# Splitting half of the embedding product of two row tiles into three fp32r products, with GpSimd making the parts

## The reference, cut to what matters

```
x = layer_norm(patches, g1, b1)          # 448 x 1024
x = x @ W + b                            # W: 1024 x 512, all float32
h = layer_norm(x, g2, b2)                # 448 x 512
h = h + attention(normalise(h))          # 16 heads of 128, causal, 7 keys each
h = h + ffn(quantise(normalise(h)))      # fp8 quantised rows, 512 x 512
```

## Time and profile before

| | |
|---|---|
| time, three runs | 265.09 us median, 264.95 to 265.5 |
| the profiled execution | 264.66 us, span 262.9 us |
| TensorE matmul (PE) | 256.3 us busy, 97% |
| TensorE weight load (PEld) | 220.1 us, 84% |
| VectorE (DVE) | 157.6 us, 60% |
| ScalarE (ACT) | 125.0 us, 48% |
| GpSimd (POOL) | 0.2 us, 0% |
| granted TensorE clock | 0.99 |
| chain of work that ended last | PE 91%, DVE 4% |
| embedding products (L353) in that chain | 10% |

### The profile page before, as it was taken

How to read it: one execution, slowest core, us unless ns; L and a number is a source line. 1 busy time by engine, 2 the same in 40 slices (tenths; PEclk the granted TensorE clock), 3 DMA queues, 4 the chain that set the end, 5 groups by cost and what they waited for, 6 DMA issues and landing times.

```text
span 262.9 us, 3852 instructions
## 1 busy us (share of the span) xinstructions
PE 256.3 (97%) x1428; PEld 220.1 (84%) x1428; DVE 157.6 (60%) x321; ACT 125.0 (48%) x216; POOL 0.2 (0%) x4
## 2 busy tenths in 40 slices
PE   8999999999899999999999999999999999999994
PEld 6444548989799999999999999999999999998772
DVE  6367887627828623942591288139623958934884
ACT  2677853635535343624363345435333642537680
POOL 0000000000000000000000000000000000000000
PEclk9999999999999999999999999999999999999898
DMA  5999120340270233052205300530320020000004
GB/s 161 358 302 372 30 91 0 99 143 0 51 271 0 89 113 120 1 168 59 92 0 199 120 0 16 184 120 0 111 89 0 2 80 0 2 0 0 0 4 140
DMA packets 7585, 23.57 MB, mean 90 GB/s; under 512 B 1251, under 2 KB 1715, under 8 KB 7446
## 3 DMA queue, kind: packets, MB, share of 16 engines
q1 hardware_dynamic: 7574, 23.42, 26.6%
HBM read 22.50 MB, written 0.92 MB: 89 GB/s over the span
## 4 chain that ended last, share of the span: by engine, by line
PE 91%; DVE 4%; DMA 1%; issue 1%; ACT 1%; SPq 0%; DVEq 0%; ACTq 0%
PE bank L312 14%; PE bank L313 14%; PE bank L314 14%; PE acc L353 10%; PE acc L454 9%; PE bank L429 5%; PE bank L438 5%; PE acc L458 4%; PE acc L648 3%; PE bank L444 3%; PE bank L421 2%; PE bank L518 2%; PE bank L336 1%; DMA x_in<-patches 1%; PE bank L634 1%; DVE stats L949 1%
## 5 line engine op out<-in xcount | busy, mean ns | idle before, releaser
L312 PE MATMUL bank<-ht_hi,qkvw_hi 128*128 128x448 f32 (+1 forms) x192 | 69.4, 362 | 0.9 <-issue 0.9
L313 PE MATMUL bank<-ht_lo,qkvw_hi 128*128 128x448 f32 (+1 forms) x192 | 69.0, 360 | 0.0
L314 PE MATMUL bank<-ht_hi,qkvw_lo 128*128 128x448 f32 (+1 forms) x192 | 69.0, 360 | 0.0
L942 DVE TENSOR_TENSOR qkvw_lo<-raw_qkv,qkvw_hi 128x1536 fp32r<-128x1536 f32 x16 | 28.1, 1754 | 35.4 <-ACT qkvw_hi L680 35.4
L312 PEld LDWEIGHTS bank<-ht_hi,qkvw_hi 128*128 128x128 f32 x192 | 36.1, 188 | 3.9 <-issue 1.2
L314 PEld LDWEIGHTS bank<-ht_hi,qkvw_lo 128*128 128x128 f32 x192 | 36.1, 188 | 2.7
L313 PEld LDWEIGHTS bank<-ht_lo,qkvw_hi 128*128 128x128 f32 x192 | 36.1, 188 | 2.6
L353 PE MATMUL acc<-tokw_raw,xt 128*112 128x512 f32 x64 | 28.6, 592 | 0.0
L680 ACT CAST qkvw_hi<-raw_qkv 128x1536 fp32r<-128x1536 f32 x16 | 23.5, 1470 | 0.0
L1112 DVE COPY prob_t<-bank 112x448 f32<-112x448 f32 x8 | 5.0, 624 | 29.0 <-PE bank L421 29.0
L353 PEld LDWEIGHTS acc<-tokw_raw,xt 128*112 128x112 f32 x64 | 10.9, 177 | 13.7 <-issue 10.6
(11 more groups left out here) (145 smaller groups left out, 395.3 us busy)
## 6 DMA issues: line engine op xcount, KB each, us to landing
raw_qkv<-heads_w SPq DMA_DIRECT2D x16, 768.0 KB, 4.3
raw_out<-heads_w SPq DMA_DIRECT2D x16, 256.0 KB, 4.5
tokw_raw<-tok_w SPq DMA_DIRECT2D x4, 512.0 KB, 6.7
x_in<-patches SPq DMA_DIRECT2D x3, 448.0 KB, 9.3
ffnw_raw<-ffn_w SPq DMA_DIRECT2D x1, 1024.0 KB, 15.3
out<-h_sb SPq DMA_DIRECT2D x3, 224.0 KB, 2.6
x_in<-patches SPq DMA_DIRECT2D x2, 224.0 KB, 2.9
g_row<-tok_g SPq DMA_DIRECT2D x1, 224.0 KB, 10.4
```

The source lines that it names most:

```text
L312: nc.tensor.matmul(ps, hi, whi, start=first, stop=False, skip_group_check=True)
L313: nc.tensor.matmul(ps, hi, wlo, start=False, stop=False, skip_group_check=True)
L314: return nc.tensor.matmul(ps, lo, whi, start=False, stop=last, skip_group_check=True)
L942: return nc.vector.tensor_tensor(dst, src, hi.bitcast(F32), ALU.subtract)
```

## The change

GpSimd gets a stream. First it makes, for chunks 4 to 7 of the embedding weights, the high part (`tensor_copy` from float32 to fp32r) and the low part (`tensor_tensor` subtract), in two steps of two chunks (1024 elements in each of 128 partitions), each step after its quarter of the weights has landed. Then, for tile 2 and tile 3, once all eight chunks of `xt` of the tile are there, it makes the high and the low part of chunks 4 to 7 of `xt` (448 elements in each of 128 partitions). Each subtraction waits for the copy before it. The parts are put into the buffers of the feed-forward's weights and activations, which are not in use before the end.

TensorE does chunks 0 to 3 of every tile, and all of tiles 0 and 1, as before. For tiles 2 and 3, from chunk 4 on, `embed_split` takes the place of the four float32 products: eight fp32r products of the high part of `xt` with the high and low parts of the weights, then four of the low part of `xt` with the high part of the weights. It waits for the high part of the patches, for each pair of weight chunks, and before the last four for the low part of the patches.

```diff
+FIRST_SPLIT, FIRST_SPLIT_TILE = 4, 2
...
+        tokw_hi, tokw_lo = ffnw_hi, ffnw_lo
+        xt_hi, xt_lo = xq_t[:, 0:2, :], xq_t[:, 2:4, :]
...
+        @block.gpsimd
+        def _(pool):
+            def split_weights(i):
+                a, b = 2 * i, 2 * i + 2
+                pool.wait_ge(tokw_landed[(FIRST_SPLIT + a) // 2], 16)
+                raw = tokw_raw[:, FIRST_SPLIT + a:FIRST_SPLIT + b, :]
+                nc.gpsimd.tensor_copy(tokw_hi[:, a:b, :], raw).then_inc(tokw_hi_ok, 1)
+                pool.wait_ge(tokw_hi_ok, i + 1)
+                nc.gpsimd.tensor_tensor(tokw_lo[:, a:b, :], raw, tokw_hi[:, a:b, :].bitcast(F32),
+                                        ALU.subtract).then_inc(tokw_lo_ok, 1)
+
+            def split_patches(t):
+                i = t - FIRST_SPLIT_TILE
+                pool.wait_ge(xt_ok, KIN * (t + 1))
+                raw = xt[:, t % 2, FIRST_SPLIT * TR:KIN * TR]
+                nc.gpsimd.tensor_copy(xt_hi[:, t % 2, :], raw).then_inc(xt_hi_ok, 1)
+                pool.wait_ge(xt_hi_ok, i + 1)
+                nc.gpsimd.tensor_tensor(xt_lo[:, t % 2, :], raw, xt_hi[:, t % 2, :].bitcast(F32),
+                                        ALU.subtract).then_inc(xt_lo_ok, 1)
+
+            for i in range((KIN - FIRST_SPLIT) // 2):
+                split_weights(i)
+            for t in range(FIRST_SPLIT_TILE, TILES):
+                split_patches(t)
...
+            def embed_split(t):
+                pe.wait_ge(xt_hi_ok, t - FIRST_SPLIT_TILE + 1)
+                for i in range(KIN - FIRST_SPLIT):
+                    if i % 2 == 0:
+                        pe.wait_ge(tokw_hi_ok, i // 2 + 1)
+                        pe.wait_ge(tokw_lo_ok, i // 2 + 1)
+                    for w in (tokw_hi, tokw_lo):
+                        nc.tensor.matmul(acc[t][0:TR, :], xt_hi[:, t % 2, i * TR:(i + 1) * TR], w[:, i, :],
+                                         start=False, stop=False, skip_group_check=True)
+                pe.wait_ge(xt_lo_ok, t - FIRST_SPLIT_TILE + 1)
+                for i in range(KIN - FIRST_SPLIT):
+                    last = nc.tensor.matmul(acc[t][0:TR, :], xt_lo[:, t % 2, i * TR:(i + 1) * TR], tokw_hi[:, i, :],
+                                            start=False, stop=(i == KIN - FIRST_SPLIT - 1), skip_group_check=True)
+                return last
+
             def embed(t, ahead_of):
                 for k in range(KIN):
...
                     pe.wait_ge(xt_ok, KIN * t + k + 1)
+                    if t >= FIRST_SPLIT_TILE and k >= FIRST_SPLIT:
+                        last = embed_split(t)
+                        break
                     last = nc.tensor.matmul(acc[t][0:TR, :], xt[:, t % 2, k * TR:(k + 1) * TR], tokw_raw[:, k, :],
                                             start=False, stop=(k == KIN - 1), skip_group_check=True)
                 last.then_inc(tok_ps, 1)
```

More of the change, by code:

```diff
@@ L144, in audio_tower @@
         tok_b_landed = sem("tok_b_landed")
+        tokw_hi_ok = sem("tokw_hi_ok")
+        tokw_lo_ok = sem("tokw_lo_ok")
+        xt_hi_ok = sem("xt_hi_ok")
+        xt_lo_ok = sem("xt_lo_ok")
         bias_cleared = sem("bias_cleared")
```

## The result

| | before | changed |
|---|---|---|
| median of 18 runs each | 265.00 us | 264.44 us |
| lowest to highest | 264.59 to 266.08 | 263.77 to 265.42 |
| ratio, with 95% interval | | 0.9971 (0.9962 to 0.998) |
| profiled execution, span | 264.66 us, 262.9 us | 264.58 us, 262.8 us |

The changed kernel is faster, by 0.8 us by the ratio (0.5 to 1.0 us by its interval). I had forecast 264.5 us and a gain of 0.6 us.

The account below looks back on a forecast made before the run. TensorE, busy 97% of the span and 91% of the chain, was taken as the bound. A gain of 1.0 us less 0.4 us for the hold on VectorE gave -0.6 us, 264.5 us against the median, range 263.9 to 265.5 us.

Parts of the forecast that it names:

- TensorE's part: Tiles 2 and 3: twelve fp32r products replace four float32 ones, saving 0.63 us a tile, 1.26 us in all.
- Rival D: On TensorE: fp32r products go at 0.29 us each, no gain, 265.2 us with a small hold; chance 0.06.
- What is late next: At tile 3's `hn_sb` transposes: only 1.0 us of 1.26 us comes through, bounds 0.6 and 1.3 us.
- the wait between the two halves: At tile 3's `hn_sb` transposes: the second pair no longer waits for the second half of `hn_sb`, estimated 0.1 us.
- its two chains: Meeting at tile 3's `hn_sb` transposes: VectorE's for tile 3, 1.26 us earlier, and TensorE's own work, 0.63 us earlier.
- GpSimd ready in time: Parts for tiles 2 and 3 are ready before TensorE wants them, with 3 to 4 us of cover; costs nothing.
- Rival C: TensorE waits at tile 2's high part because GpSimd is too slow: +2.5 us, 267.6 us; chance 0.07.
- The hold on VectorE: GpSimd delays VectorE's small operations on tile 2's patches (17.38 to 17.99 us): 0.4 us lost, bounds 0 and 1.7.
- rival A: The hold on VectorE at tile 2's patches costs nothing: -1.0 us, 264.1 us; chance 0.31.
- B: Full hold on VectorE; TensorE stops about 1.0 us at tile 2's patch transposes: 0.0, about 265.1 us; chance 0.20.
- The sum: Whole kernel: -1.0 us for TensorE's saving and +0.4 us for the hold give -0.6 us.

Follow-up runs that it names:

- x1: Changed kernel with only tile 2 split into fp32r products, tile 3 as before: 264.76 us, 0.9983 of the kernel before.
- x2: Changed kernel with only tile 3 split into fp32r products, tile 2 as before: 264.98 us, 0.999 of the kernel before.
- x7: Changed kernel with the nine residual transposes moved ahead of tile 2's `hn_sb` transposes: 263.87 us, 0.9961 of the kernel before.
- x9: Changed kernel with GpSimd's weight steps gated, residual transposes first, and tile 3's root ahead of ScalarE's copy for tile 2: 263.56 us, 0.9958 of before.
- x4: Changed kernel with GpSimd's weight steps waiting so that none runs while VectorE makes a patch `nmr`: 264.28 us, 0.9961 of the kernel before.
- x5: The changed kernel run once more, unedited: 264.28 us, 0.9979 of the kernel before.
- x11: Kernel before, no GpSimd work, with residual transposes first, root first and tile 2's patches loaded earlier: 265.35 us, 1.001 of the kernel before.
- x3: Changed kernel where GpSimd does all its splitting but TensorE keeps the float32 products: 265.22 us, 1.0006 of the kernel before.
- x10: Changed kernel plus tile 1 split, gated weight steps, residual transposes and root first, tile 2's patches before the last weights: 263.51 us, 0.994 of before.
- x6: Changed kernel with one more GpSimd copy (616 elements) between the two weight steps: 264.59 us, 0.9988 of the kernel before.

## Why the prediction was right, point by point

**TensorE's part.** Forecast 0.61 to 0.67 us for each tile, by 0.231 us a product; 0.67 us read at tile 2, products at 0.23 us. Right. Rival D is out.

**What is late next.** The stop ahead of tile 2's `hn_sb` transposes was forecast at 0.7 us and is 0.65 us; x1 and x2 show that the two tiles are worth 0.68 and 0.32 us, where the forecast had 0.63 us and the rest of 1.0. Tile 3's transposes were forecast 0.9 us earlier and are 0.97 and 0.98 us earlier, counted from P1. The last products of the first head (47.13 us before, 46.51 us in the changed kernel) were forecast 1.0 us earlier and are: 32.51 us behind P1 before, 31.51 us now. The 0.1 us for the wait between the two halves was not there (the row of the four transposes went from 0.64 to 0.61 us). But one of its two chains was wrong: I had VectorE's for tile 3 1.26 us earlier. It starts 1.3 us earlier, counted from P1, and ends 1.0 us earlier, as it waits for a root on ScalarE that stands behind a copy, and the copy waits for the transposes of tile 2 that stand behind the very stop I had predicted. I had followed what TensorE's stop does to TensorE's own work and not to the queue of the engine that it feeds. That the number came out all the same is luck: TensorE's own work, the chain I had right, was as late. x7 is where the error showed, and x9, which moves the root, is its proof.

**GpSimd ready in time.** Forecast 1.0 to 2.0 us for the copy, 1.2 to 2.3 us for the subtraction, weights done between 16.3 and 20.6 us: 1.04 and 2.39 us, done at 18.9 us. The subtraction lies just above my upper end. No product waited. Rival C is out.

**The hold on VectorE.** Forecast 0.4 us between 0 and 1.7. That it exists is shown by seven profiled executions with it and by x4, where it is gone. The Trainium skill (SBUF — State Buffer, "Who interferes with whom") says that the second of the two "fully blocks" until the first is done, and the traces agree: the held operation ended 0.01 to 0.02 us behind GpSimd's in all seven. The slack that covers it was forecast at 1.3 us and is 4.59 - 3.37 = 1.22 us. Its price is 0 in the two profiles of the changed kernel (rival A); over the six profiles with the weight steps as in the change it is 0, 0, 0, 0.21, 0.40 and 0.43 us, 0.2 us in the mean, half of the forecast. The times would allow the 0.4 us of the forecast and cannot show it: by the medians x5 is 0.3 us worse than x4, but the intervals overlap, and x7, which has the hold, has x4's ratio. B, a stop of 1.0 us, appeared in none. What I had not seen is what sets the price: where GpSimd's last weight step ends against P1, which depends on when the third quarter of the weights lands (the first copy started between 11.65 and 12.76 us) and on how early TensorE is. The prediction's reckoning with a subtraction of 2.25 us had the last one end at 18.8 to 20.0 us and `nmr` 0.6 us behind it; in the six profiles it ended at 18.60 to 19.72 us, and `nmr` 0.40 us behind. Only one of the three small operations was held, since between two GpSimd operations VectorE gets in (its `nmr` ended at 13.00 us, with GpSimd's copy over at 12.99 us and its subtraction not begun before 13.07 us) and the second subtraction was the last of the weight steps.

**The sum.** -0.6 us forecast, -0.56 us by the medians of 18 runs, -0.77 us by the ratio. What stays open is how the mean splits: -1.0 us of the stage and +0.2 to +0.4 us of the hold fit both figures, but the interval (0.5 us wide) would just fit no hold at all.

## What to carry to other kernels

A saving on the engine that sets the pace is worth its full size only up to the next meeting with a chain that was level with it; follow the stop that then appears into the queue of every engine that waits for it: here a root stood behind a copy. Work given to an idle engine can hold a busy one even when its own result is never late: look in VectorE's chains for short operations with two operands from the on-chip memory, and start GpSimd's long ones behind them. What such a hold costs depends on when the long operation ends, so trace that end back to the load that released it. And when two profiles differ by less than their noise, compare a stage between landmarks, not the span.

## What the runs showed of the hardware that was not expected

- The head loop, the same instructions in all kernels, took 142.2 us in eight of the fourteen profiled executions and 142.6 us in the other six. In the changed kernel one pair of heads takes it all, 24.89 us in place of 24.5 us, with the granted clock at 1.00 in that stretch (126 to 151 us). In the other five one pair takes 24.88 us as well, and not always the same pair. What causes it no run here shows. These are the rows of the probability transposes in the chain of the changed kernel:

```profile
101.41 0.77 PE bank L472 x8
125.91 0.77 PE bank L472 x8
150.80 0.77 PE bank L472 x8
175.32 0.77 PE bank L472 x8
```

- The kernel's first 8 us differ as well: in the changed kernel two weight loads of the first bias products last 0.31 us each and not 0.18 us, and the patch transposes of tile 0 start 0.4 us later; in x5, with the same program, too, in x1 not. It is so in x11 as well, which has no work on GpSimd, so it isn't the change's doing. The granted clock reads 1.00 there as well.
- From 248 to 250 us the granted clock read 0.50 (the level of 1.2 GHz) in the profile of before and 1.00 in that of the changed kernel; the part behind the head loop took 39.72 and 39.46 us. Such a stretch at 0.50 is in five of the fourteen profiles, those of before, x1, x3, x4 and x10, with 39.62 to 40.11 us for that part; the nine others took 39.42 to 39.49 us. From 244 to 246 us TensorE was busy 1.76 us in before and 1.77 us in the changed kernel, so its activity just ahead of the fall does not tell the two apart.
- A GpSimd subtraction of 1024 elements with two float32 operands took 2.36 to 2.41 us in every run, 2.3 ns for an element, and one of 448 elements 1.14 to 1.16 us, 2.6 ns. A rounding copy of 1024 elements took 1.03 to 1.07 us and one of 448 elements 0.55 to 0.60 us; the plain copy of 616 elements in x6 took 0.70 us.
- Not every VectorE operation with two operands is held. The centring of tile 2 at 33.26 us of the changed kernel, with one operand in PSUM and one in SBUF (the on-chip memory in which the held operations have both), lies inside GpSimd's subtraction of tile 3's patches (32.82 to 33.97 us) for most of its length and takes 0.75 us, as before the change (VectorE's row of the changed kernel):

```profile
33.26 0.75 DVE L1065 SCALAR_TENSOR_TENSOR hn_sb<-acc,moments,g_row 112x512 f32<-112x512 f32 x1
```
